# Role-conditioned adapter on one core: batch 0 first, with its own role's weights, and the array goes through the head batch by batch

## What is computed

```python
h = jnp.einsum('bsh,bhk->bsk', hidden_states, W_down[role]) + b_down[role][:, None, :]
h = jax.nn.gelu(h, approximate=False)
u = jnp.einsum('bsk,bkh->bsh', h, W_up[role]) + b_up[role][:, None, :]
y = hidden_states + u
mean = jnp.mean(y, axis=-1, keepdims=True)
var = jnp.mean(jnp.square(y - mean), axis=-1, keepdims=True)
yn = (y - mean) * jax.lax.rsqrt(var + LN_EPS)
return yn * gamma[role][:, None, :] + beta[role][:, None, :]
```

## Time and profile before

| what | value |
|---|---|
| median of 3 runs | 1417.38 us (1417.31 to 1417.69) |
| the profiled execution | 1416.96 us |
| its span in the profile | 1415.2 us |
| PE busy in it | 1401.1 us, 99% |
| DVE, ACT, POOL busy | 85%, 55%, 14% |
| DMA | 283.49 MB, 200 GB/s over the span |
| first matmul of a product | 12.17 us after the start |
| last matmul begins | some 8 us before the end |

### The profile page before, as it was taken

How to read it: one execution, slowest core, us unless ns; L and a number is a source line. 1 busy time by engine, 2 the same in 40 slices (tenths; PEclk the granted TensorE clock), 3 DMA queues, 4 the chain that set the end, 5 groups by cost and what they waited for, 6 DMA issues and landing times.

```text
span 1415.2 us, 29331 instructions
## 1 busy us (share of the span) xinstructions
PE 1401.1 (99%) x6175; PEld 1158.2 (82%) x6176; DVE 1204.8 (85%) x1458; ACT 776.8 (55%) x2047; POOL 201.0 (14%) x300
## 2 busy tenths in 40 slices
PE   8999999999999999999999999999999999999997
PEld 6888888888888888888888888888888888888886
DVE  8798988888888888888888899988888888888887
ACT  5555555555555555555555555555555555555555
POOL 4376311100000000000000377311100000000000
PEclk9999999999999999999999999999999999999999
DMA  8677777766566666665666778777765666656654
GB/s 230 183 225 241 215 212 200 211 195 198 184 195 199 194 184 196 200 192 184 194 200 193 213 227 234 222 198 201 218 199 185 196 200 190 185 194 199 192 186 149
DMA packets 208868, 283.49 MB, mean 200 GB/s; under 512 B 25791, under 2 KB 155584, under 8 KB 208846
## 3 DMA queue, kind: packets, MB, share of 16 engines
q1 hardware_dynamic: 201438, 269.34, 61.4%
q0 software_dynamic: 5888, 12.07, 4.6%
q10 hardware_dynamic: 1520, 1.84, 0.4%
HBM read 183.27 MB, written 99.88 MB: 200 GB/s over the span
## 4 chain that ended last, share of the span: by engine, by line
PE 98%; DVE 1%; DMA 1%; issue 0%; ACT 0%; DVEq 0%; ACTq 0%
PE p_up L1120 16%; PE p_up L1118 16%; PE p_up L1119 16%; PE p_down L1118 16%; PE p_down L1120 16%; PE p_down L1119 16%; DMA row<-in_L_cond_W_down 0%; DMA x_quad<-in_x 0%; DVE row L1038 0%; PE p_hT L1114 0%; DVE row L866 0%; DMA w_raw<-in_itok_B 0%; DVE x_quad L820 0%; DVE wd_lo L758 0%; DVE x_quad L1024 0%
## 5 line engine op out<-in xcount | busy, mean ns | idle before, releaser
L1118 PE MATMUL p_down<-wd_hi,xT_hi 128*128 x1012 | 393.9, 389 | 0.7 <-DVE xT_lo L782 0.4
L1120 PE MATMUL p_down<-wd_hi,xT_lo 128*128 x1012 | 393.7, 389 | 0.0
L1119 PE MATMUL p_down<-wd_lo,xT_hi 128*128 x1012 | 393.7, 389 | 0.0
L1118 PE MATMUL p_up<-wu_hi,hT_hi 128*128 x1008 | 392.3, 389 | 0.0
L1120 PE MATMUL p_up<-wu_hi,hT_lo 128*128 x1008 | 392.1, 389 | 0.0
L1119 PE MATMUL p_up<-wu_lo,hT_hi 128*128 x1008 | 392.1, 389 | 0.0
L595 ACT ACTIVATE hT_hi<-p_hT 128x512 fp32r<-128x512 f32 x126 | 75.7, 601 | 381.5 <-DVE p_hT L800 378.9
L820 DVE SCALAR_TENSOR_TENSOR row<-p_up,row 128x1024 f32<-128x1024 f32 x126 | 154.2, 1224 | 126.3 <-PE p_up L1120 126.2
L581 ACT ACTIVATE xT_hi<-xT_raw 128x1024 fp32r<-128x1024 f32 x125 | 132.8, 1062 | 187.6 <-PE p_down L1120 185.6
L1118 PEld LDWEIGHTS p_down<-wd_hi,xT_hi 128*128 128x128 f32 x1012 | 189.6, 187 | 40.8 <-issue 1.4
L1119 PEld LDWEIGHTS p_down<-wd_lo,xT_hi 128*128 128x128 f32 x1012 | 190.3, 188 | 39.7
(11 more groups left out here) (174 smaller groups left out, 981.3 us busy)
## 6 DMA issues: line engine op xcount, KB each, us to landing
x_quad<-in_x SPq DMA_DIRECT2D x510, 128.0 KB, 3.4
row<-in_x SPq DMA_DIRECT2D x126, 512.0 KB, 4.0
out<-row SPq DMA_DIRECT2D x126, 512.0 KB, 2.7
h_dram<-h SPq DMA_DIRECT2D x125, 256.0 KB, 4.1
h_quad<-h_dram SPq DMA_DIRECT2D x498, 64.0 KB, 1.9
w_raw<-in_L_cond_W_down POOLq DMA_DIRECT2D x64, 64.0 KB, 3.2
w_raw<-in_L_cond_W_up POOLq DMA_DIRECT2D x64, 64.0 KB, 3.6
row<-in_L_cond_W_up SPq DMA_DIRECT2D x16, 128.0 KB, 3.6
```

Source lines behind the costliest of these rows:

```text
L1118: pe.matmul(dst, a_hi, w_hi, start=first, stop=False)
L1119: pe.matmul(dst, a_hi, w_lo, start=False, stop=False)
L1120: return pe.matmul(dst, a_lo, w_hi, start=False, stop=last)
```

## The change

Batch 0 is always the first (its key is raised by 4 x 128), and its role is the first role. So x of batch 0 is loaded without waiting for anything, while the weights wait for the role numbers: SP and ACT each read batch 0's role (`role_of_first`) and issue halves of pieces 0, 1 and 2, then x of the second batch, then piece 3. The parameter rows of all three roles are loaded (21 rows instead of 7, in two copies), by SP, ACT and POOL, and a selector made from the role picks the wanted ones. ACT copies them (`rows`), where DVE did. The sort runs on all partitions and no longer needs PE for the keys. It is moved behind the splits of batch 1 on DVE (`sort_all`), and the order is turned into a row by PE after batch 1. PE starts with filler matmuls of 256 columns (`keep_clock`), does all of batch 0, with the spreads between, and then all of batch 1. The bias of batch 0 is added by PE (`spread(p_down[:, :], 0, False)`), and ACT takes the gelu from PSUM (`gelu_first`).

The core of the diff:

```diff
         @block.sync
-            sp.dma_start(role_row, role.rearrange("(o b) -> o b", o=1)).then_inc(roles_loaded, 16)
+            sp.dma_start(role_row, role.partition_broadcast(P)).then_inc(roles_loaded, 16)
+            load_x0(sp, range(0, NQ // 2))
             sp.wait_ge(param_rows_clear, 1)
-            for at in (0, LOW):
...
+            load_param_rows(sp, beta_rows, BETA_ROW, param_rows_loaded)
+            load_param_rows(sp, beta_rows, LOW + BETA_ROW, param_rows_loaded)
+            first_role = role_of_first(sp)
+            for n in range(3):
+                load_first(sp, first_role, n, range(0, NQ // 2))
...
             sp.wait_ge(first_known, 1)
-            for b, quads in ((0, range(0, NQ // 2)), (1, range(NQ))):
-                load_quads(sp, sp.value_load(first_numbers[0:1, b:b + 1], min_val=0, max_val=B - 1), b, quads)
-            load_first(sp, FD - 2, range(NQ // 2, NQ))
-            load_first(sp, FD - 1)
-            sp.wait_ge(numbers_ready, 1)
-            load_x(2)
+            load_quads(sp, numbers[1], 1, range(0, NQ // 2))
+            load_first(sp, first_role, 3, range(0, NQ // 2))
+            sp.wait_ge(x_transposed, 1)
+            load_quads(sp, numbers[2], 0)
             for n in range(FD, FD + FU):
                 sp.wait_ge(first_split, n - RING + 1)
-                load_first(sp, n)
-            load_x(3)
+                load_first(sp, first_role, n)
+            sp.wait_ge(x_transposed, 2)
+            load_quads(sp, numbers[3], 1)
+            sp.wait_ge(numbers_ready, 1)
         @block.gpsimd
+            pool.memset(wu_lo[:, 0:FILL].bitcast(F32), 1.0).then_inc(filler_ready, 1)
...
+            load_param_rows(pool, gamma_rows, LOW + GAMMA_ROW, more_rows_loaded)
+            load_param_rows(pool, up_bias_rows, UP_BIAS_ROW, more_rows_loaded)
+            load_param_rows(pool, up_bias_rows, LOW + UP_BIAS_ROW, more_rows_loaded)
         @block.scalar
-            load_first(act, 0, range(0, 1))
+            load_x0(act, range(NQ // 2, NQ - 1))
             act.wait_ge(out_ready, 1)
             act.activation(factor[:, 0:1], opener[:, 2:3], ACT.Gelu)
-            load_first(act, 0, range(1, NQ))
-            load_first(act, 1)
+            load_x0(act, range(NQ - 1, NQ))
+            act.wait_ge(param_rows_clear, 1)
+            load_param_rows(act, b_down, 0, param_rows_loaded)
+            load_param_rows(act, b_down, LOW, param_rows_loaded)
+            load_param_rows(act, gamma_rows, GAMMA_ROW, param_rows_loaded)
+            first_role = role_of_first(act)
+            for n in range(3):
+                load_first(act, first_role, n, range(NQ // 2, NQ))
...
+            act.wait_ge(param_rows_loaded, 16 * 5)
+            act.wait_ge(more_rows_loaded, 16 * 3)
+            act.activation(rows, rows_raw, ACT.Copy).then_inc(param_rows_hi, 1)
+            round_half(0, 0)
+            load_quads(act, numbers[1], 1, range(2, 3))
             round_first(0)
+            load_quads(act, numbers[1], 1, range(3, 4))
+            round_half(0, 1)
+            load_first(act, first_role, 3, range(2, 3))
             round_first(1)
...
         @block.vector
+            subtract_half(0, 0)
             split_first(0)
+            split_chunk(1, 0, chunk_split)
+            split_chunk(1, 1, first_split)
+            subtract_half(0, 1)
+            split_first(2)
+            transpose_half(1, 0)
+            split_first(3)
+            subtract_half(1, 0)
+            transpose_half(1, 1)
+            subtract_half(1, 1)
+            sort_all()
+            transpose_half(2, 0)
+            transpose_half(2, 1)
+            subtract_half(2, 0)
         @block.tensor
+            pe.wait_ge(filler_ready, 1)
+            keep_clock(18)
+            pe.wait_ge(first_known, 2)
...
+            keep_clock(10)
...
+            first_product().then_inc(half_down, 1)
+            second_product().then_inc(down_done, 1)
             pe.wait_ge(pieces_split, when_split[1])
             half_product(1, 0, other, weights_at[1]).then_inc(half_down, 1)
-            half_product(0, 1, p_down[:, :], weights_at[0]).then_inc(down_done, 1)
             half_product(1, 1, other, weights_at[1]).then_inc(down_done, 1)
+            pe.wait_ge(order_ready, 1)
+            pe.wait_ge(gelu_done, 1)
+            pe.matmul(p_up[0][0:1, 2 * B:3 * B], number_col[:, :], onehot, start=True, stop=True).then_inc(order_in_psum, 1)
             turn_h(0)
```

More of the change, by code:

```diff
@@ L120, in adapter_kernel @@
         table = sb("table", [1, NUMBER + B + 8], I32)
-        ones_row, ident = h_quad[0:1, 0, :], h_quad[:, 1, :]
+        index_row, ident, onehot, key = h_quad[:, 0, :].bitcast(I32), *(h_quad[:, n, :] for n in range(1, 4))
         first_keys = sb("first_keys", [1, 8], I32)
@@ L1066, in _ @@
         def _(pe):
-            pe.wait_ge(key_ready, 1)
-            pe.matmul(p_up[0][:, 0:B], ones_row, key, start=True, stop=True)
-            pe.matmul(p_up[0][:, B:B + 1], key, ones_row[:, 0:1], start=True, stop=True).then_inc(key_spread, 1)
-            pe.wait_ge(first_known, 2)
             weights_reg = [pe.alloc_register(f"weights_at{n}") for n in range(RING)]
@@ L1156, in body, with hi_by_hi @@
                     mm.then_inc(up_done, 1)
-            def half_product(b, half, dst, at):
-                hi, lo = half_x(b, half)
-                for c in range(half * HALF, half * HALF + HALF):
-                    if (b, c) == (0, FC // K):
-                        pe.wait_ge(chunk_split, 1)
-                    elif (b, c) == (0, FC // K + 1):
-                        pe.wait_ge(first_split, 2)
-                    elif b == 0 and c % (FC // K) == 0:
-                        pe.wait_ge(first_split, c // (FC // K) + 1)
-                    mm = product(dst, hi[:, c % HALF, :], lo[:, c % HALF, :], cols(wd_hi, at + c * K, K),
-                                 cols(wd_lo, at + c * K, K), c == 0, c == HC - 1)
-                return mm
+            def hi_by_hi(b, half, dst, at, chunks):
+                hi, _ = half_x(b, half)
+                for c in chunks:
+                    pe.matmul(dst, hi[:, c % HALF, :], cols(wd_hi, at + c * K, K), start=c == 0, stop=False)
@@ new lines, in hi_by_lo, with lo_by_hi @@
+            def hi_by_lo(b, half, dst, at, chunks):
+                hi, _ = half_x(b, half)
+                for c in chunks:
+                    mm = pe.matmul(dst, hi[:, c % HALF, :], cols(wd_lo, at + c * K, K), start=False, stop=c == HC - 1)
+                return mm
+            def lo_by_hi(b, half, dst, at, chunks):
+                _, lo = half_x(b, half)
+                for c in chunks:
+                    mm = pe.matmul(dst, lo[:, c % HALF, :], cols(wd_hi, at + c * K, K), start=False, stop=False)
+                return mm
```

265 lines of the change are left out of this document (148 added, 117 removed).

## The result

The changed kernel takes **1421.7 us** (median of 7 runs, 1420.51 to 1423.17), the one before took 1417.31 in the same comparison: ratio 1.0032, 95% interval 1.0020 to 1.0043. By the median that is slower by 0.32%; the interval's lower end is 0.20%. The forecast of 1418.0 was 3.7 us too low, and its range ended at 1420.0.

What follows compares the result with a forecast made beforehand. DMAs were taken to bound the head: piece 3 complete at 15.7 plus 8.6 us put `turn_h(0)` at 24.3 against 23.75, +0.55 us, all else costed at nothing. On the median of 1417.38 that gave 1418.0 us, range 1416.1 to 1420.0.

Steps and rivals of the forecast that it cites:

- The role numbers land at 0.86 + 1.26 = 2.12: Head: the role load, issued at 0.86, takes 1.26 us, so the numbers are there at 2.12 us.
- Say 3.1, and bytes 1 us later: Head: weights are issued from 3.1 us and their bytes flow from 4.1.
- the DMAs don't run dry: Head, before the weights flow: the queue has 0.68 MB to move until 4.6 us, so no hole in transfers.
- x of batch 2 behind it on SP's queue: Head: batch 2's x follows piece 3 of W_down, so only 3.30 MB stand ahead of that piece's end.
- rival C: Head: parameter rows, waiting for POOL's DMAs, hold ACT's rounds; rows at 9.4 us give 1419.6; chance 0.18.
- The rate: Head: DMAs move 250 GB/s, so 3.30 MB take 13.2 us and piece 3 is complete at 15.7.
- rival B: Head: two queues at once move 280 GB/s, piece 3 at 14.3, total 1416.5 us; chance 0.19.
- From piece 3 to the turn: Head, from piece 3's completion to the start of `turn_h(0)`: 2.8 + 5.58 + 0.2, in sum 8.6 us.
- ACT ready for piece 3: Head: ACT and DVE need 8.0 us from the rows' arrival at 7.7, so ACT can round piece 3 at 15.7.
- PE idles for some 2 us: Head, before piece 3: this idle time covers seven spreads, the bias by PE and 28 filler matmuls, costed at nothing.
- Rival D, the clock: Head: waiting for piece 3 drops PE to 1.2 GHz, adding 1.5 us, to 1419.5; chance 0.05.
- The change leaves that loop ... and the program's end alone.: Loop from batch 3 on and program's end: no change in time, so only the head counts.

Runs made afterwards that it cites:

- e3: Kernel before with lower bounds on waited-for registers, plus its role numbers loaded to 128 partitions instead of one; 1420.58 us.
- e13: Changed kernel with lower bounds, SP's load of batch 2's x moved behind the first two pieces of W_up; 1420.86 us.
- e7: Changed kernel with lower bounds, roles also loaded to one partition first, short sort for the first batches, piece 3 ahead of batch 1's x; 1420.17 us.
- e11: e10 with piece 3 put back where the change had it; 1421.03 us.
- e2: Changed kernel with lower bounds, batch 0's role fetched first by its own 32-byte DMA to one partition; 1420.51 us.
- e10: e7 with 36 filler matmuls instead of 18; 1421.31 us.
- e6: Changed kernel with lower bounds, piece 3 issued right behind the first three by SP and ACT, ahead of batch 1's x; 1422.94 us.
- e14: e10 with batch 2's x behind two pieces of W_up, and piece 3 rounded and split before batch 1's x is turned; 1418.20 us.
- e1: Changed kernel with only lower bounds added on the registers that DVE and PE wait for; 1422.19 us.
- e4: e1 with 36 filler matmuls instead of 18 ahead of first_known; 1422.22 us.
- e5: Kernel before with only the lower bounds on the registers that two engines wait for; 1418.22 us.
- e9: Changed kernel with lower bounds, batch 0's x and POOL's parameter rows waiting until the roles are spread; 1424.68 us.
- e8: Kernel before with lower bounds, roles to one partition, then 127 different 512 B rows of x to the others, the sort waiting for both; 1422.87 us.
- e12: e10 with weights issued ahead of parameter rows on SP and ACT, and ACT's quarters of pieces 2 and 3 issued by POOL; 1424.49 us.
- e15: e14 with 52 filler matmuls in place of 36; 1418.29 us.
- e16: e15 with 60 filler matmuls; 1418.58 us.

## Why the prediction was wrong, point by point

**The failing step** is "The role numbers land at 0.86 + 1.26 = 2.12". I took 1.26 from the row of a load to one partition and used it for a load to 128, although I counted the 0.066 MB of it in the bytes. Measured: 3.90, landing at 4.76. e3 shows that this alone costs the old kernel 2.4 us. The trace of before had no row for such a load, so by my own method it needed two ends. The nearest rows for a load of many packets, 3.2 to 4.9, would have put the numbers 1.9 to 3.6 us later, and the turn's shift, one for one, at 2.5 to 4.2 instead of 0.55. It was 3.0. Of the 3.9 us by which the profiled span exceeds the forecast, 2.5 are in this shift and 1.5 in the loop and at the end. That one load explains the whole shift so closely is partly luck: the next points have errors of about the same size that cancel.

**"Say 3.1, and bytes 1 us later"; "the DMAs don't run dry".** Weights were issued at 5.7, and between 6 and 7 us the DMAs moved 68 GB/s. The 0.54 MB missing by 7 us are 2.2 us at 250 GB/s, as much as piece 3 was late (17.86 for 15.7).

**"x of batch 2 behind it on SP's queue", and so not in the 3.30 MB.** Wrong for ACT's half of piece 3, which is issued between roundings, at 10.45 and 11.53, when SP is already issuing batch 2's x. 0.57 MB more were moved by then, and e13 gives 1.3 us for taking them away. I had named this in rival C and let it fall as small.

**The rate** came out better than forecast, 289 GB/s from 7 to 15 against 250: rival B was right there. The 3.12 MB that moved from 7 us to the landing took 10.9 us, at 250 GB/s it would be 12.5: those 1.6 us hid most of what the 0.57 MB cost (2.3 at 250 GB/s). With the 0.6 us that the forecast added for the landing, and that the measured 3.87 MB already contain, the sum is 2.2 + 2.3 - 1.6 - 0.6 = 2.3, against 2.2 measured. Over the whole stretch from 2 to 15 us, which includes the hole, it was 234.

**From piece 3 to the turn**: 8.6 forecast, 26.76 - 17.86 = 8.9 measured. **ACT ready for piece 3** 8.0 us behind its first copy: 17.36 - 9.23 = 8.1. Both hold. But the first copy was at 9.23, not 7.7, because ACT was issuing weights until 8.7 and then loaded the first numbers, known since 8.05, into registers. So rival C was right that ACT comes late (its 9.4 gave 1419.6), by another cause than POOL's rows; in e7 and e11, where ACT waits for those rows, they are there at 8.4 and 7.8. The lower ends that I used for them, 6.3 in rival B and 5.9 in the bounds, lie under my own low end of 6.7 and have no row.

**"PE idles for some 2 us" before piece 3**, the cover for what I costed at nothing, was not there: 0.15 us. With a first product at 11.58, half clock until 13.9 and seven spreads among the products, PE itself was a second limit next to the DMAs. That is why e2, e7, e10 and e13, which each left some limit in place, gained 0.9 to 2.0 of the 4.0 us, why e6 lost 0.75, and why only e14, which moved all but PE's own work, came back to the old level, with the help of a shorter loop and end.

**Rival D, the clock.** I argued from the earlier trace rows that 2 us of idle are short, and from the same rows that 5 us kept the full clock. In e1 PE went back to half clock at 8.4, within an idle stretch of 3.65 us, and in e10 at 20.4, 1.3 us behind one of 1.93. By the Trainium skill (TensorE: Matmul & The Clock Gate, Part 1) idleness closes the gate and only sustained work opens it again. e1's rows agree: the clock was 0.50 from 9 to 15 us, with PE busy for 5.7 of these 6, and full only from 15.2. My rows of the end kept the full clock for 5 us of idle and e1's lost it within 3.65, so one such stretch doesn't tell what the next will do. The half clock cost nothing in the changed kernel (e4), since piece 3 would have held PE.

**"The change leaves that loop ... and the program's end alone."** The instructions, yes; the time grew by 0.65 and 0.83 us. e5 shows the same wait and 0.37 us of the longer end in the old order. The end is 9.34 to 9.39 in after, e1, e4, e6 and e9, 9.00 in e2 and e13, 8.87 to 8.88 in e3, e5 and e8, and 8.58 to 8.66 in e7, e10, e11, e12, e14, e15 and e16. So it is short wherever the loop's wait is missing; what links the two stays open.

## What to carry to other kernels

A number that decides where all later loads go is worth a DMA of its own, to one partition, ahead of the copy for every partition; and a load's price must be read from a row of the same shape, packets and all, before anything is put behind it. When a head has several limits close together (a late number, an engine that issues DMAs between its computations, bytes of a later batch in flight, an array at half clock), single repairs look worthless: list them all, and test them together as well as one by one. And a small edit, here a few register operations, can move a background engine into another rhythm, which costs some tenths in a loop that nobody touched. So compare stage by stage, and look which execution a profile shows before you set it beside a median.

## What the runs showed of the hardware

- A DMA of 64 KB as 128 rows of 512 B took 2.89 us alone (e9), 1.5 of them from its first packet to its last, and 3.5 to 4.1 us beside other loads. One row of 512 B took 1.26. A DMA of 127 such rows took 5.72 (e8), its packets in single file.
- A small transfer behind large ones comes as late as they do: 12 KB took 7 us in e12. The third issuing queue there brought no bandwidth either, 279 GB/s from 9 to 12 us against 327 in e7 with two. The Trainium skill (DMA: Bandwidth & Descriptors, Issuing engines are not separate DMA queues) says that all queues run on the same 16 DMA engines and that several of them only save issue time. The trace agrees.
- DVE operations with both inputs in SBUF stretch beside POOL's: 2.14 us for L874 at 89.47, 1.22 for the same line at 100.89. The Trainium skill (SBUF — State Buffer, SBUF: two separate sides) describes a port pair that one of the two engines holds for a whole instruction while the other waits. The trace agrees: the three operations shown above were longer by 0.92, 0.40 and 1.03 us, and POOL's operation had 1.06, 0.55 and 1.22 us to go when they began, so each waited for nearly all of what was left.
- The clock column can read 1.00 where PE ran at half clock. In the trace of after it is 1.00 from the start, while matmuls of 512 columns start 0.43 us apart until 13.9 and 0.23 after; in e1's trace it is 0.50 from 8.4 to 15.2. The distance of the matmuls decides.
